# Gated expert stages: a tile's second product and the copy of its rows come one step later

## The chip, the cores and the metric

One core of one Trainium2 chip runs the whole program. The metric is the device time of one execution in microseconds; the kernel before has a median of 1701.94 us over three runs (1701.4 to 1706.82). Times inside the program come from one further execution, recorded by the hardware profiler.

## The reference

x is 32 x 128 tokens of 128 features, with a context of the same size. Four layers follow each other, each an attention over the context and then a mixture of eight experts, each added to x:

```python
x = x + _L0_xattn_ref(ctx_1024, _layernorm(x), ...)
x = x + _L0_ffn_ref(_layernorm(x), ...)      # top 2, GELU
x = x + _L1_xattn_ref(...)
x = x + _L1_ffn_ref(...)                     # top 2, gated, 256 rows an expert
x = x + _L2_xattn_ref(...)
x = x + _L2_ffn_ref(...)                     # top 2, gated
x = x + _L3_xattn_ref(...)
x = x + _L3_ffn_ref(...)                     # top 1, GELU
```

The two gated layers compute, for a token's row x and each chosen expert e, a product with two 128 x 256 matrices, a gate, and a product with a 256 x 128 matrix; the results of the chosen experts are mixed with the router's weights:

```python
# layer 1
y = a * (b * jax.nn.sigmoid(b)) @ W_out[e]   # a = xin @ W[e], b = xin @ V[e]
# layer 2
hidden = jax.nn.silu(gate_out) * up_out      # halves of x @ gate_up_w[e]
expert_out = hidden @ down_w[e]
```

## The kernel before

Rows are sorted by expert first, so that an expert stage works on tiles of 128 rows that all belong to one expert. `experts(layer)` (L1413) is that stage for all four layers. Layers 1 and 2 are `gated`. Layer 1 is also `fixed`: 16 tiles, two an expert, all indices known when the program is built. Layer 2 has up to 71 tiles (`n_tiles`), and which expert a tile belongs to is read from a table at run time, so its steps stand in a loop of eight, with a few steps written out before and behind (`run`, L1444).

The stage is a software pipeline, written out by hand as one function `step(k, u)` for each engine, where u is the slot of tile k among eight. Engines run by themselves and meet at semaphores; each works through its own program in order. In step k:

- PE (TensorE) turns the rows of tile k+2 (`turn_rows`, L1544, banks 0 and 1 of PSUM), makes the first product of tile k+1 (`hidden`, L1554, four matmuls of 128 x 128 in fp32, each seen as two records, into banks 2 and 3 or 4 and 5), and the second product of tile k (`rows_out`, L1566, two matmuls, four records, bank 6 or 7). Ahead of the first product it waits for DVE's copies of the tile's turned rows and of the expert's weights; ahead of the second for the gated features (`hidden_kept`) and for ACT's copy of the rows of two tiles before (`expert_kept`).
- ACT (ScalarE) applies Silu to the first half of tile k+1's first product (L1583) and then copies the finished rows of tile k-1 out of PSUM (L1594) into one of eight slots.
- DVE (VectorE) copies the turned rows of tile k+2 (L1626), in layer 2 the 128 x 512 weights of its expert into `tile_w1` (L1628), and then multiplies gate and second half of tile k+1 into `hidden` (L1633). In layer 1 it has preparations for the next attention in the same step (L1640, L1648).
- POOL (GpSimd) issues an indirect DMA for each tile that scatters its rows to DRAM (L1528). In layer 1 it also issues the indirect DMA that gathers a tile's rows (L1523), the gather of tile j ahead of the scatter of tile j-6. At the end it waits until all scatters have landed.
- SP (SyncE) in layer 2 loads the rows of tile j (L698), after the scatter of tile j-8 has landed, since that one reads its row numbers from the same slot. Ahead of the loads from tile 8 on stands a 2 MB load of the turned context (L1495).

The next stage's block starts when all engines have finished this one. Layers 0 and 3 use the same functions with four matmuls for the second product and GELU in place of the gate.

The order in PE's step and the two waits ahead of the second product:

```python
def step(k, u):
    turn_rows(k + 2, (u + 2) % SLOTS)
    hidden(k + 1, (u + 1) % SLOTS)
    rows_out(k, u)
...
pe.wait_ge(hidden_kept.sem, j + (hidden_kept.value + 1))
if beyond(j, 2):
    pe.wait_ge(expert_kept.sem, j + (expert_kept.value - 1))
```

Of the kernel before, what the change touches and what calls it, by code (L numbers as in the profile page):

```python
# [13 lines left out]
ALU = mybir.AluOpType  # L14
# [9 lines left out]
P = 128  # L24
# [4 lines left out]
H1 = 512  # L29
# [85 lines left out]
def build(nc, A, out):  # L115
    with ExitStack() as top:
# [1296 lines left out]
        def experts(layer):  # L1413
# [4 lines left out]
            NC = 2 if gated else 4  # L1418
            WIDE = H1 if gated else HB
            PARTS = 2  # L1420
            UNROLL = SLOTS
            LAG = 6
            scatters = layer in SCATTERED
# [3 lines left out]
            with ExitStack() as ph:  # L1427
# [1 line left out]
                xt = sb_in(ph, "tile_turned", [P, 2, P])  # L1429
                w1 = sb_in(ph, "tile_w1", [P, 4, WIDE])  # L1430
                gat = sb_in(ph, "gate", [P, 2, 2 * P])
                hidT = sb_in(ph, "hidden", [P, 2, NC * P])
                yo = sb_in(ph, "expert_rows_sb", [P, SLOTS, P])
                b2 = sb_in(ph, "expert_b2", [P, E * P])
                ctx_stats = sb_in(ph, "ctx_stats", [P, B, 6])
# [8 lines left out]
                def run(eng, step):  # L1444

                    if fixed:
                        for k in range(-2, n_tiles + 1):
                            step(k, k % UNROLL)
                        return
                    for k in range(-2, 2):  # L1450
                        step(k, k % UNROLL)
                    with eng.Fori(0, (n_tiles - 4) // UNROLL) as q:
                        for u in range(UNROLL):
                            step(q * UNROLL + (2 + u), (2 + u) % UNROLL)
                    for k in range(2 + (n_tiles - 4) // UNROLL * UNROLL, n_tiles + 1):
                        step(k, k % UNROLL)

                def in_slot(s):
# [8 lines left out]
                def slot_is_free(eng, j, s):  # L1467
                    if isinstance(j, int):
                        if j >= SLOTS:
                            eng.wait_ge(expert_out[s].sem, expert_out[s].value + 16 * (j // SLOTS))  # L1470
                    else:
                        eng.wait_ge(expert_out[s].sem, (j - s) * (16 // SLOTS) + expert_out[s].value)

                def hidden_bank(s, half):
                    return bank[2 + 2 * (s % 2) + half]
# [58 lines left out]
                def _(pe):  # L1534
# [11 lines left out]
                    def hidden(j, u):  # L1546
                        if exists(j):
                            pe.wait_ge(rows_turned_kept.sem, j + (rows_turned_kept.value + 1))
                            if not fixed:
                                pe.wait_ge(weights_placed.sem, j + (weights_placed.value + 1))  # L1550
                            for n in range(4):
                                c = (n + 2) % 4 if fixed else n
                                w = W1[:, (j // 2) * H1 + c * P:(j // 2) * H1 + (c + 1) * P] if fixed else w1[:, u % 4, c * P:(c + 1) * P]
                                ins = pe.matmul(hidden_bank(u, n // 2)[:, n % 2 * P:(n % 2 + 1) * P], w, xt[:, u % 2, :], start=True, stop=True)  # L1554
                                if n % 2:
                                    ins.then_inc(hidden_made.sem, 1)

                    def rows_out(j, u):
                        if exists(j):
                            off = expert_of(pe, j) * (NC * P)  # L1560
                            pe.wait_ge(hidden_kept.sem, j + (hidden_kept.value + 1))
                            if beyond(j, 2):
                                pe.wait_ge(expert_kept.sem, j + (expert_kept.value - 1))
                            out_ = bank[6 + u % 2]
                            for c in range(NC):
                                ins = pe.matmul(out_[:, 0:P], hidT[:, u % 2, c * P:(c + 1) * P], W2[:, bass.ds(off + c * P, P)],  # L1566
                                                start=(c == 0), stop=(c == NC - 1))
                            ins.then_inc(expert_made.sem, 1)

                    def step(k, u):  # L1570
                        turn_rows(k + 2, (u + 2) % SLOTS)
                        hidden(k + 1, (u + 1) % SLOTS)
                        rows_out(k, u)
                    run(pe, step)

                @block.scalar
                def _(act):
                    def step(k, u):
                        j, s = k + 1, (u + 1) % SLOTS
                        if exists(j):  # L1580
# [3 lines left out]
                            else:  # L1584
                                for c in range(NC):
                                    if c % 2 == 0:
                                        act.wait_ge(hidden_made.sem, j * PARTS + (hidden_made.value + 1 + c // 2))
                                    ins = act.activation(hidT[:, s % 2, c * P:(c + 1) * P], hidden_bank(s, c // 2)[:, c % 2 * P:(c % 2 + 1) * P], ACT.Gelu, bias=w1[:, s % 4, H1 + c:H1 + c + 1])  # L1588
                                ins.then_inc(hidden_kept.sem, 1)
                        j, s = k - 1, (u - 1) % SLOTS  # L1590
                        if gated and exists(j):
                            act.wait_ge(expert_made.sem, j + (expert_made.value + 1))
                            slot_is_free(act, j, s)
# [11 lines left out]
                def _(dve):  # L1605
# [8 lines left out]
                    def step(k, u):  # L1614
# [7 lines left out]
                        if exists(j):  # L1622
# [3 lines left out]
                            dve.tensor_copy(xt[:, s % 2, :], bank[s % 2][:, 0:P]).then_inc(rows_turned_kept.sem, 1)  # L1626
                            if not fixed:
                                dve.tensor_copy(w1[:, s % 4, :], W1[:, bass.ds(off, WIDE)]).then_inc(weights_placed.sem, 1)  # L1628
                        j, s = k + 1, (u + 1) % 2
                        if gated and exists(j):  # L1630
                            dve.wait_ge(gates_kept.sem, j + (gates_kept.value + 1))
                            dve.wait_ge(hidden_made.sem, j * PARTS + (hidden_made.value + 2))
                            dve.tensor_tensor(hidT[:, s, :], hidden_bank(s, 1)[:, 0:2 * P], gat[:, s, :], ALU.mult).then_inc(hidden_kept.sem, 1)  # L1633
                        if fixed and exists(k):
                            if k < QUARTERS * len(HEAD_PARTS):
                                whole, parts = HEAD_PARTS[k // QUARTERS]
# [1225 lines left out]
```

## Time and profile before

| what | value |
|---|---|
| median of three runs | 1701.94 us |
| lowest and highest | 1701.4 and 1706.82 us |
| profiled execution, first to last instruction | 1769.0 us |
| PE busy (share of the span) | 1426.5 us (81%) |
| PE weight loads busy | 1315.8 us (74%) |
| DVE busy | 1112.7 us (63%) |
| ACT busy | 892.0 us (50%) |
| POOL busy | 768.7 us (43%) |
| mean granted TensorE clock | 0.878 |

The profiled execution's span is the only time given of it; it is longer than the timed runs. Shares of busy time are means over stages that have different limits: the two gated stages are 51 us and some 145 us of the span. How a row is read: a group or a timeline row names the line of the kernel, the engine, the operation, what it writes and what it reads. "PEld" are PE's weight loads, which run beside its matmuls. Idle time is the engine's time with nothing running ahead of the row, and the arrow says whose semaphore came last. Starts are in us from the first instruction. A number of underscores behind a tile's name tells the stages apart: `hidden_` is layer 1, `hidden__` layer 2.

### The profile page before, as it was taken

The numbers are of one execution on the slowest core, as the hardware profiler recorded it, in microseconds if no ns is written. First come the engines' busy times: TensorE is split into PE (matmuls) and PEld (weight loads), VectorE is DVE, ScalarE is ACT, GpSimd is POOL, SyncE is SP. The second block draws the span as 40 slices with busy tenths as digits, with TensorE's granted clock in tenths as the row PEclk, the third lists the DMA queues.
The fourth block names the chain that finished last, engine by engine and source line by source line (L and its number), as shares of the span: only waits on it lengthen the run. The fifth ranks groups of instructions, "written<-read, shape, count | busy, mean of one in ns | idle before, by whom it ended". The sixth has DMA issues, their size and how long they took to land. (4 is left out here: it accounts for less than half of the span.)

```text
span 1769.0 us, 37485 instructions
## 1 busy us (share of the span) xinstructions
PE 1426.5 (81%) x10866; PEld 1315.8 (74%) x10867; DVE 1112.7 (63%) x3494; ACT 892.0 (50%) x2683; POOL 768.7 (43%) x764
## 2 busy tenths in 40 slices
PE   6665779975677569999999999999993999366494
PEld 4554579964556459999999999999992888154494
DVE  5634544438766457777777778787875455585343
ACT  4443135541223148777777777777771222243252
POOL 3064424430002545565656565666453455005342
PEclk9886779995576879999999999999997999677697
DMA  9311112213022130000000000000001322601224
GB/s 232 19 37 36 40 50 64 64 47 139 24 95 59 39 97 11 13 1 18 9 17 7 16 7 16 7 4 7 5 9 41 110 70 68 198 1 36 66 63 121
DMA packets 94444, 87.05 MB, mean 49 GB/s; under 512 B 17108, under 2 KB 81079, under 8 KB 93959
## 3 DMA queue, kind: packets, MB, share of 16 engines
q1 hardware_dynamic: 75240, 56.44, 12.1%
q0 software_dynamic: 11936, 24.55, 4.2%
q10 hardware_dynamic: 7168, 4.86, 1.0%
q8 instruction: 47, 0.77, 0.2%
q14 instruction: 53, 0.43, 0.1%
HBM read 54.03 MB, written 33.35 MB: 49 GB/s over the span
## 5 line engine op out<-in xcount | busy, mean ns | idle before, releaser
L2159 POOL TENSOR_TENSOR paired_rows<-paired_rows,rinv 128x1024 f32<-128x1024 f32 x128 | 242.4, 1894 | 245.1 <-DVE rinv L2474 230.3
L2465 DVE TENSOR_TENSOR probs_turned_lo<-psum_banks,probs_turned_hi 128x512 fp32r<-128x512 f32 x256 | 175.7, 686 | 141.9 <-ACT probs_turned_hi L2324 118.8
L2350 ACT ACTIVATE paired_rows<-psum_banks,neg_max 128x256 f32<-128x256 f32 x512 | 236.7, 484 | 1.1 <-DVEq L2051 0.4
L2271 PE MATMUL psum_banks<-probs_turned_hi,y_rows 128*128 128x256 f32 x1024 | 213.8, 292 | 0.9 <-DVEq L2051 0.9
L2221 PE MATMUL psum_banks<-y_turned_parts,queries_hi 128*128 128x256 f32 x1024 | 198.7, 292 | 3.0 <-DVEq L2051 3.0
L2271 PEld LDWEIGHTS psum_banks<-probs_turned_hi,y_rows 128*128 128x128 f32 x1024 | 167.1, 189 | 1.7 <-DVEq L2051 1.5
L2324 ACT CAST probs_turned_hi<-psum_banks 128x512 fp32r<-128x512 f32 x256 | 151.2, 591 | 20.4 <-PE psum_banks L2192 10.5
L2192 PE MATMUL psum_banks<-ident,paired_rows 128*128 128x128 f32 x1024 | 155.9, 275 | 6.9 <-DVE probs_turned_lo L2465 4.5
L2221 PEld LDWEIGHTS psum_banks<-y_turned_parts,queries_hi 128*128 128x128 f32 x1024 | 157.2, 190 | 3.5 <-issue 3.5
L2480 DVE TENSOR_REDUCE neg_max<-psum_banks 128x4 f32<-128x1024 f32 x128 | 155.5, 1215 | 5.5 <-PE psum_banks L2221 3.5
L2221 PE MATMUL psum_banks<-y_turned_parts,queries_lo 128*128 128x256 f32 x512 | 144.3, 282 | 0.0
L2271 PE MATMUL psum_banks<-probs_turned_lo,y_rows 128*128 128x256 f32 x512 | 144.2, 282 | 0.0
L2324 ACT CAST queries_hi<-psum_banks 128x512 fp32r<-128x512 f32 x128 | 74.9, 585 | 107.0 <-PE psum_banks L2257 94.9
L2192 PEld LDWEIGHTS psum_banks<-ident,paired_rows 128*128 128x128 f32 x1024 | 115.3, 140 | 11.9 <-DVE probs_turned_lo L2465 3.5
L1528 POOL DMA_INDIRECT expert_rows<-expert_rows_sb,tile_rows x71 | 70.9, 998 | 104.9 <-DVE expert_rows_sb L1620 104.9
L1588 ACT ACTIVATE hidden<-psum_banks,tile_w 128x128 f32<-128x128 f32 x284 | 81.2, 368 | 69.6 <-PE psum_banks L1554 69.6
L2350 ACT ACTIVATION_READ_ACCUMULATOR paired_rows<-psum_banks,neg_max 128x1 f32 x512 | 110.0, 215 | 0.0
L2257 PE MATMUL psum_banks<-y_turned_parts,wqk_hi 128*128 128x256 f32 x512 | 104.0, 296 | 0.8 <-POOL y_turned_parts L2083 0.8
L1528 POOL DMA_INDIRECT expert_rows<-expert_rows_sb__,tile_rows x71 | 68.3, 962 | 77.1 <-ACT expert_rows_sb__ L1594 64.8
L2271 PEld LDWEIGHTS psum_banks<-probs_turned_lo,y_rows 128*128 128x128 f32 x512 | 97.2, 190 | 0.0
L2221 PEld LDWEIGHTS psum_banks<-y_turned_parts,queries_lo 128*128 128x128 f32 x512 | 97.0, 189 | 0.0
L745 POOL DMA_INDIRECT rows_by_expert_first<-paired_rows,top_experts x64 | 62.1, 970 | 76.9 <-DVE top_experts L1123 45.0
(698 smaller groups left out, 3781.4 us busy)
## 6 DMA issues: line engine op xcount, KB each, us to landing
paired_rows<-expert_rows SPq DMA_DIRECT2D x16, 512.0 KB, 6.0
tile_rows<-rows_by_expert SPq DMA_DIRECT2D x110, 64.5 KB
tile_rows<-rows_by_expert_first SPq DMA_DIRECT2D x71, 64.5 KB
expert_w_b<-in_L_ffn_w_dram SPq DMA_DIRECT2D x2, 2048.0 KB, 12.9
tile_rows<-expert_rows SPq DMA_DIRECT2D x8, 512.0 KB
x_rows<-in_x_dram SPq DMA_DIRECT2D x8, 256.0 KB, 5.2
ctx_turned_dram<-ctx_turned SPq DMA_DIRECT2D x1, 2048.0 KB, 10.4
normed_rows_dram<-paired_rows SPq DMA_DIRECT2D x1, 2048.0 KB, 8.7
```

Source lines behind the costliest of these rows:

```text
L745: pool.indirect_dma_start(xfirst, bass.IndirectOffsetOnAxis(ap=first_spots[:, i, k, t:t + 1], axis=0), ROWS[:, i * N + t, :], None).then_i ...
L1528: pool.indirect_dma_start(ys, bass.IndirectOffsetOnAxis(ap=to, axis=0), yo[:, i % SLOTS, :], None).then_inc(expert_out[i % SLOTS].sem, 16)
L1588: ins = act.activation(hidT[:, s % 2, c * P:(c + 1) * P], hidden_bank(s, c // 2)[:, c % 2 * P:(c % 2 + 1) * P], ACT.Gelu, bias=w1[:, s % 4 ...
L2159: ins = pool.tensor_tensor(probs[:, k, :, :], probs[:, k, :, :], rinv[:, k, :].unsqueeze(2).to_broadcast([P, 4, 256]), ALU.mult)
L2192: ins = pe.transpose(bank[T_BANK][:, h * P:(h + 1) * P], probs[:, par, h, c * P:(c + 1) * P], ident[:, :])
L2221: ins = pe.matmul(bank[S_BANKS[par] + r][:, h * 256:(h + 1) * 256], queries[q][:, h, r, :], yparts[:, 2 * s2 + y, r * 256:(r + 1) * 256], ...
L2257: ins = pe.matmul(bank[Q_BANK][:, h * 256:(h + 1) * 256].rearrange("p (r q) -> p r q", r=2), wqk_parts[w][:, 2 * u3 + h, :], latents_of, s ...
L2271: ins = pe.matmul(bank[Z_BANK][:, r * 256:(r + 1) * 256], yrows[:, 2 * s1 + y, (2 * r + k) * P:(2 * r + k + 1) * P], probsT[x][:, (u + 1) ...
L2324: ins = act.copy(dst, bank[bank_][:, :])
L2350: ins = act.activation(probs[:, par, h, :], bank[S_BANKS[par] + h // 2][:, (h % 2) * 256:(h % 2 + 1) * 256], ACT.Exp, bias=nmax[:, par, h: ...
L2465: ins = dve.tensor_tensor(lo, bank[bank_][:, :], hi.bitcast(F32), ALU.subtract)
L2480: ins = dve.tensor_reduce(nmax[:, par, :], ps[:, S_BANKS[par]:S_BANKS[par] + 2, :].rearrange("p r (h k) -> p (r h) k", k=256), AX.X, ALU.m ...
```

## The change

For the gated layers PE's step k makes the second product of tile k-1 (it was k), and ACT's step copies the rows of tile k-2 (it was k-1). The gated features get four buffers (two before), and the first product of tile j waits in addition for the gated features of tile j-2 to be made, since the second product, by which this was ensured, no longer stands ahead of it. The stage has one step more at its end. Layers 0 and 3 keep their order and their waits.

```diff
--- before.py
+++ after.py
@@ -1418,6 +1418,7 @@
             NC = 2 if gated else 4
             WIDE = H1 if gated else HB
             PARTS = 2
+            BEHIND = 1 if gated else 0
             UNROLL = SLOTS
             LAG = 6
             scatters = layer in SCATTERED
@@ -1429,7 +1430,7 @@
                 xt = sb_in(ph, "tile_turned", [P, 2, P])
                 w1 = sb_in(ph, "tile_w1", [P, 4, WIDE])
                 gat = sb_in(ph, "gate", [P, 2, 2 * P])
-                hidT = sb_in(ph, "hidden", [P, 2, NC * P])
+                hidT = sb_in(ph, "hidden", [P, 2 + 2 * BEHIND, NC * P])
                 yo = sb_in(ph, "expert_rows_sb", [P, SLOTS, P])
                 b2 = sb_in(ph, "expert_b2", [P, E * P])
                 ctx_stats = sb_in(ph, "ctx_stats", [P, B, 6])
@@ -1444,7 +1445,7 @@
                 def run(eng, step):
 
                     if fixed:
-                        for k in range(-2, n_tiles + 1):
+                        for k in range(-2, n_tiles + 1 + BEHIND):
                             step(k, k % UNROLL)
                         return
                     for k in range(-2, 2):
@@ -1452,7 +1453,7 @@
                     with eng.Fori(0, (n_tiles - 4) // UNROLL) as q:
                         for u in range(UNROLL):
                             step(q * UNROLL + (2 + u), (2 + u) % UNROLL)
-                    for k in range(2 + (n_tiles - 4) // UNROLL * UNROLL, n_tiles + 1):
+                    for k in range(2 + (n_tiles - 4) // UNROLL * UNROLL, n_tiles + 1 + BEHIND):
                         step(k, k % UNROLL)
 
                 def in_slot(s):
@@ -1470,6 +1471,9 @@
                             eng.wait_ge(expert_out[s].sem, expert_out[s].value + 16 * (j // SLOTS))
                     else:
                         eng.wait_ge(expert_out[s].sem, (j - s) * (16 // SLOTS) + expert_out[s].value)
+
+                def hidden_slot(s):
+                    return s % (2 + 2 * BEHIND)
 
                 def hidden_bank(s, half):
                     return bank[2 + 2 * (s % 2) + half]
@@ -1548,6 +1552,8 @@
                             pe.wait_ge(rows_turned_kept.sem, j + (rows_turned_kept.value + 1))
                             if not fixed:
                                 pe.wait_ge(weights_placed.sem, j + (weights_placed.value + 1))
+                            if BEHIND and beyond(j, 2):
+                                pe.wait_ge(hidden_kept.sem, j + (hidden_kept.value - 1))
                             for n in range(4):
                                 c = (n + 2) % 4 if fixed else n
                                 w = W1[:, (j // 2) * H1 + c * P:(j // 2) * H1 + (c + 1) * P] if fixed else w1[:, u % 4, c * P:(c + 1) * P]
@@ -1563,14 +1569,14 @@
                                 pe.wait_ge(expert_kept.sem, j + (expert_kept.value - 1))
                             out_ = bank[6 + u % 2]
                             for c in range(NC):
-                                ins = pe.matmul(out_[:, 0:P], hidT[:, u % 2, c * P:(c + 1) * P], W2[:, bass.ds(off + c * P, P)],
+                                ins = pe.matmul(out_[:, 0:P], hidT[:, hidden_slot(u), c * P:(c + 1) * P], W2[:, bass.ds(off + c * P, P)],
                                                 start=(c == 0), stop=(c == NC - 1))
                             ins.then_inc(expert_made.sem, 1)
 
                     def step(k, u):
                         turn_rows(k + 2, (u + 2) % SLOTS)
                         hidden(k + 1, (u + 1) % SLOTS)
-                        rows_out(k, u)
+                        rows_out(k - BEHIND, (u - BEHIND) % SLOTS)
                     run(pe, step)
 
                 @block.scalar
@@ -1585,9 +1591,9 @@
                                 for c in range(NC):
                                     if c % 2 == 0:
                                         act.wait_ge(hidden_made.sem, j * PARTS + (hidden_made.value + 1 + c // 2))
-                                    ins = act.activation(hidT[:, s % 2, c * P:(c + 1) * P], hidden_bank(s, c // 2)[:, c % 2 * P:(c % 2 + 1) * P], ACT.Gelu, bias=w1[:, s % 4, H1 + c:H1 + c + 1])
+                                    ins = act.activation(hidT[:, hidden_slot(s), c * P:(c + 1) * P], hidden_bank(s, c // 2)[:, c % 2 * P:(c % 2 + 1) * P], ACT.Gelu, bias=w1[:, s % 4, H1 + c:H1 + c + 1])
                                 ins.then_inc(hidden_kept.sem, 1)
-                        j, s = k - 1, (u - 1) % SLOTS
+                        j, s = k - 1 - BEHIND, (u - 1 - BEHIND) % SLOTS
                         if gated and exists(j):
                             act.wait_ge(expert_made.sem, j + (expert_made.value + 1))
                             slot_is_free(act, j, s)
@@ -1626,11 +1632,11 @@
                             dve.tensor_copy(xt[:, s % 2, :], bank[s % 2][:, 0:P]).then_inc(rows_turned_kept.sem, 1)
                             if not fixed:
                                 dve.tensor_copy(w1[:, s % 4, :], W1[:, bass.ds(off, WIDE)]).then_inc(weights_placed.sem, 1)
-                        j, s = k + 1, (u + 1) % 2
+                        j, s = k + 1, (u + 1) % SLOTS
                         if gated and exists(j):
                             dve.wait_ge(gates_kept.sem, j + (gates_kept.value + 1))
                             dve.wait_ge(hidden_made.sem, j * PARTS + (hidden_made.value + 2))
-                            dve.tensor_tensor(hidT[:, s, :], hidden_bank(s, 1)[:, 0:2 * P], gat[:, s, :], ALU.mult).then_inc(hidden_kept.sem, 1)
+                            dve.tensor_tensor(hidT[:, hidden_slot(s), :], hidden_bank(s, 1)[:, 0:2 * P], gat[:, s % 2, :], ALU.mult).then_inc(hidden_kept.sem, 1)
                         if fixed and exists(k):
                             if k < QUARTERS * len(HEAD_PARTS):
                                 whole, parts = HEAD_PARTS[k // QUARTERS]
```

## Rows read from the trace of the kernel before

**Rows 1.** Busy time in two stretches: layer 1, layer 2's steady part; last clock, DMA.
```profile
562.00:613.00 51.00, 32.67 (x208) 29.07 (x208) 25.65 (x117) 14.40 (x41) 32.69 (x32) 0.82 0.14 41
1390.00:1503.00 113.00, 103.97 (x795) 93.23 (x794) 62.63 (x183) 33.05 (x123) 58.19 (x61) 1.00 0.25 70
```

**Rows 2.** Groups of lines, 1390 to 1503 us; busy, mean ns, then idle before, releasers.
```profile
L1554 PEld LDWEIGHTS psum_banks<-tile_turned__,tile_w__ 128*128 128x128 f32 x489 | 59.4, 191 | 9.7 <-DVE tile_w__ L1628 6.8 <-issue 2.6
...
L1566 PEld LDWEIGHTS psum_banks<-paired_rows,hidden__ 128*128 128x128 f32 x244 | 31.9, 190 | 9.3 <-issue 7.6
```

**Rows 3.** Timeline of PE, layer 2, two unstalled steps: start, length, what.
```profile
1411.72 1.06 PE L1554 MATMUL psum_banks<-tile_turned__,tile_w__ 128*128 128x128 f32 x8
...
1413.17 1.06 PE L1554 MATMUL psum_banks<-tile_turned__,tile_w__ 128*128 128x128 f32 x8
```

**Rows 4.** Timeline of all engines, layer 2, a stalled step.
```profile
1438.96 1.16 PE L1554 MATMUL psum_banks<-tile_turned__,tile_w__ 128*128 128x128 f32 x8
...
1440.81 1.06 PE L1554 MATMUL psum_banks<-tile_turned__,tile_w__ 128*128 128x128 f32 x8
1442.10 0.42 DVE L1633 TENSOR_TENSOR hidden__<-psum_banks,gate__ 128x256 f32<-128x256 f32 x1 [1.57 <-PE psum_banks L1554]
...
1442.77 0.71 PE L1566 MATMUL psum_banks<-paired_rows,hidden__ 128*128 x4 [0.91 <-DVE hidden__ L1633]
...
1443.12 0.44 DVE L1628 COPY tile_w__<-expert_w_a 128x512 f32 x1
...
1443.62 1.16 PE L1554 MATMUL psum_banks<-tile_turned__,tile_w__ 128*128 128x128 f32 x8
```

**Rows 5.** Groups of lines, layer 1, 562 to 613 us.
```profile
L1566 PEld LDWEIGHTS psum_banks<-expert_w_b,hidden_ 128*128 128x128 f32 x64 | 10.0, 222 | 7.1 <-DVE hidden_ L1633 3.9 <-issue 3.3
```

**Rows 6.** Instructions of L1566, whole span: duration ns min, median, max.
```profile
L1566 PEldq FUSED_REGOPS  x582: 46/46/65, 240.8 to 1743.3; - x194
```

**Rows 7.** Timeline, end of layer 2 and start of the next stage.
```profile
1505.52 0.38 ACT L1583 ACTIVATE gate__<-psum_banks 128x256 f32<-128x256 f32 x1 [2.10 <-PE psum_banks L1554]
...
1506.33 0.96 POOL L1528 DMA_INDIRECT expert_rows<-expert_rows_sb__,tile_rows  x1 [1.67 <-ACT expert_rows_sb__ L1594]
...
1508.86 0.95 POOL L1528 DMA_INDIRECT expert_rows<-expert_rows_sb__,tile_rows  x1 [0.30 <-DMA expert_rows<-expert_rows_sb__,tile_rows]
1517.54 0.31 SPq L2614 DMA_DIRECT2D mask_row<-mask_rows  x1
```

**Rows 8.** Timeline, end of layer 1: the first and last of three scatters.
```profile
609.48 0.96 POOL L1528 DMA_INDIRECT expert_rows<-expert_rows_sb_,pair_rows  x1 [0.93 <-ACT expert_rows_sb_ L1594]
...
612.00 0.95 POOL L1528 DMA_INDIRECT expert_rows<-expert_rows_sb_,pair_rows  x1 [0.30 <-DMA expert_rows<-expert_rows_sb_,pair_rows]
```

**Rows 9.** Timeline, start of layer 1: first two copies, first scatter.
```profile
573.19 0.26 ACT L1594 COPY expert_rows_sb_<-psum_banks 128x128 f32<-128x128 f32 x1
...
573.73 1.48 POOL L1528 DMA_INDIRECT expert_rows<-expert_rows_sb_,pair_rows  x1 [2.30 <-ACT expert_rows_sb_ L1594]
...
574.23 0.26 ACT L1594 COPY expert_rows_sb_<-psum_banks 128x128 f32<-128x128 f32 x1
```

**Rows 10.** Timeline, layer 2: scatters, loads, and turns of tiles 8 and 39.
```profile
1376.78 0.96 POOL L1528 DMA_INDIRECT expert_rows<-expert_rows_sb__,tile_rows  x1 [12.33 <-ACT expert_rows_sb__ L1594]
...
1378.23 0.96 POOL L1528 DMA_INDIRECT expert_rows<-expert_rows_sb__,tile_rows  x1 [0.49 <-issue]
...
1384.03 2.67 SPq L698 DMA_DIRECT2D tile_rows<-rows_by_expert  x3
...
1385.92 0.43 PE L1544 MATMUL psum_banks<-ident,tile_rows 128*128 128x128 f32 x1 [2.12 <-DMA tile_rows<-rows_by_expert]
...
1437.73 0.96 POOL L1528 DMA_INDIRECT expert_rows<-expert_rows_sb__,tile_rows  x1 [1.42 <-ACT expert_rows_sb__ L1594]
...
1440.12 0.33 SPq L698 DMA_DIRECT2D tile_rows<-rows_by_expert  x1
...
1445.19 0.27 PE L1544 MATMUL psum_banks<-ident,tile_rows 128*128 128x128 f32 x1
```

## The prediction

> **What bounds the kernel now.** I read the page first: span 1769.0 us, PE busy 81%. The slices show two kinds of stretch; the change touches only the gated expert stages, layer 1 (16 tiles, about 562 to 613 us) and layer 2 (71 tiles, about 1369 to 1510 us), so I cut the trace there. The windows show layer 2 in its steady part at full granted clock with PE busy 104.0 of 113 us, and layer 1 with PE busy 32.7 of 51 us beside POOL at 32.7 [rows 1]. PE "busy" is not the measure here: I counted tiles. The groups of lines give 244 second products of the steady part of layer 2, four a tile, so 61 tiles in 113 us, 1.85 us each; the weight loads sat idle 9.7 us before the first product (L1554) and 9.3 us before the second (L1566) [rows 2]. Where nothing stalls, PE starts the first product every 1.45 us [rows 3], which is 13 passes (one turn, eight, four) back to back. So 61 tiles need 88 us and about 24 us are lost. Half of what is visible stands ahead of L1566, the wait that the change aims at.
>
> Then the timeline of one bad step [rows 4]. The first product of tile 35 starts at 1438.96 and of tile 36 at 1440.81, both without a stall; but DVE gets to tile 35's gated multiply only at 1442.10, released by PE, 2 us after the modelled end of the matmuls that it reads. PE stands before L1566 until 1442.77 (0.91 idle, released by DVE's hidden). Then DVE copies the next turned rows and, at 1443.12, the next expert's weights (0.44), and the first product of tile 37 starts at 1443.62, behind that copy.
>
> The matmul end that this row shows is no measured end: the Trainium skill, "Perfetto Trace Analysis", section Tensor Engine Instruction, says that the profiler computes it from size and that the semaphore follows the write's acknowledgement. The row agrees (1440.12 modelled, reader at 1442.10).
>
> **Own time and the timed runs.** The page gives the profiled execution 1769.0 us between first and last instruction; the runs without a profile have a median of 1701.94 (1701.4 to 1706.82), 67 us less. Late completions such as the one above are my candidate for part of that; then layer 2 runs nearer to 1.45 us a tile when timed, and there is less to win than the trace shows. I work out the difference in the trace's time and put it on the median.
>
> **The change, part by part.**
>
> 1. Second product one step later (L1561 to L1568). In PE's order the step was: turn k+2, first product k+1, second product k; now the last is that of k-1, whose gated features are a whole step old. The wait for DVE's hidden goes: at most 9.3 us before L1566 in layer 2 and 7.1 us in layer 1 [rows 2, 5]. What is late next? DVE works in order: multiply of tile k, turned rows of k+2, weights of k+2. None of these moves. In [rows 4] the multiply at 1442.10 is released by the first product, not by the second; from it to the end of the weights copy is 1443.12 + 0.44 - 1442.10 = 1.46 us, while PE's released second product plus turn ask 4 + 1 of the 13 passes, 0.56 us, after a multiply of 0.42 and a wake-up of 0.25 (1442.52 to 1442.77), 1.23 us in all. So when the multiply is late, the first product of k+2 is later still by 0.2 to 0.3 us, whatever PE did before. If the second product of 34 runs at 1441.7 instead, PE just stands 1.1 us longer before L1554 and starts tile 37 at 1443.62 all the same. Bounds for the gain in layer 2: 0 (all taken over by the weights wait) and 9.3 us; I take 0, since the row measured is this very case. In layer 1 the same with the turned rows in place of the weights, and there POOL paces the stage (two indirect DMAs a tile, one every 1.26 us as in rows 8, so 2.5 us a tile against PE's 1.45): bounds 0 and 7.1, taken 0.
>
> 2. The added wait in hidden() on hidden_kept of j-2. It guards the two banks of the first product. DVE did that multiply before it placed the weights of j (rows of j in layer 1), for which PE waits on the line before, so it never ends last. Queued behind it is PE's whole stream. Price: one or two sequencer operations, 46 ns each of the kind seen at L1566 [rows 6]; 0 if the sequencer is ahead of the array, 0.09 x 87 = 8 us if it is not. In the unstalled steps the matmuls follow each other without a gap [rows 3], so I take 0.
>
> 3. ACT's copy one step later. ACT's step is gate k+1, then the copy, now of k-2. The copy waits for nothing new; PE's second product still waits for a copy that stands behind the same gate as before, so its bank wait is neither better nor worse. But the scatter on POOL waits for the copy. At the end this is on the path: in layer 2 gate 70 at 1505.52 is followed by the copy of 68, and three scatters stand from 1506.33 to 1508.86, one every 1.26, and the next stage starts at 1517.54 only after the last has landed [rows 7]. Now the copy of 67 is behind that gate too: four scatters in a row instead of three, +1.26 us. Bounds 0 (if the last product came later than the queue) and 1.26; I take 1.26, because the queue is what is waited for.
>
> 4. The same at layer 1's end: three scatters from 609.48 to 612.00 behind gate 15 become four, +1.26 [rows 8]. At its start POOL idles 2.30 us for the first copy (573.19) before scatter 0; the second copy is at 574.23, and that is where the first now stands: POOL +1.04 [rows 9]. Behind scatter 0 in POOL's order is the gather of tile 7, which PE reaches several us later. If POOL is saturated to the end, the 1.04 carries through and the 1.26 does not; if not, the reverse. I take 1.3 for layer 1; bounds 0 and 2.3.
>
> 5. SP's loads in layer 2 wait for the scatter of eight tiles before. Scatter 0 goes from 1376.78 to about 1378.23, where scatter 1 stood; load 8 was issued at 1384.03, and the turn of tile 8 at 1385.92 waited for it with PE idle 2.12 us [rows 10]. The 2 MB copy of the turned context fills the DMA engines between, and scatter 1 was home by the time SP came to load 9 (1.2 us later). So 0 to 1.2 us, taken 0.3. In steady state a load follows its scatter by 2.39 us (1437.73 to 1440.12) and lands in 1.89 (1384.03 to 1385.92): 4.3 us needed [rows 10]. The turn of tile 39 was at 1445.19 [rows 10], 7.5 us after scatter 31; less one tile (1.85) leaves 5.6. Hidden, at this pace.
>
> 6. Four buffers for the features: 2 KB more a partition and no instruction; 0.
>
> Sum: 0 + 0 + 1.26 + 1.3 + 0.3 = **+2.9 us**, 1771.9 in the trace's time, **1704.8 us** for the median. That is 0.17%, under the 0.3% (5.1 us) that a measurement of this kernel can tell from no change.
>
> **Rivals.**
>
> A. *The wait removed pays.* For: 9.3 us stand before L1566, as many as before L1554, and the multiply that releases it is one of the longest steps. Against: the takeover shown in rows 4. If layer 2's 9.3 come off in full, 2.9 - 9.3 = -6.4: 1695.5 us; with layer 1's 7.1 as well 1688.4. The Trainium skill, "Trainium Kernel Development and Optimization", section Best Practices, speaks for it: consistent bubbles can mean that SBUF or PSUM ran out, and here buffers go from two to four. The trace agrees on bubbles, and names a copy, not a buffer, for those before L1554; by the page the time would be this rival's.
>
> B. *The slot cycle decides (slower).* Place: eight row slots of layer 2, scatter k, load k+8, turn k+8. The 7.46 us of part 5 are four tiles of 1.85; at 1.45 a tile they are 5.85, and less one tile 4.4, against 4.3 needed. Point of decision: a pace below about 1.45 us, or a landing only 0.1 us slower. Short by 0.45 over three remaining tiles is 0.15 a tile, x 63 = 9.5; with the 2.9, 1714 us. For: the timed runs are faster than the trace. Against: in the trace PE never waits for a load after tile 8.
>
> C. *PE's sequencer*: part 2's 8 us, with 2.9: 1712 us.
>
> D. *The order does nothing* and the ends hide behind the drain of the block: 1702 us.
>
> **How the numbers follow.** Chances: forecast 0.50 (of which 0.03 beyond 0.3%), D 0.03, A 0.24, B 0.18, C 0.05. Faster 0.24; same 0.47 + 0.03 = 0.50; slower 0.03 + 0.18 + 0.05 = 0.26. The forecast's own range is 1700 to 1708 (bounds of parts 3 to 5). For 8 in 10 it reaches to the middle of A and of B: 1692 to 1714.
>
> **What would show it.** Right: idle before L1566 in layer 2 falls towards 1 us, idle before L1554 grows by about as much, the period stays at 1.85; four scatters in a row at both ends. Wrong: a steady part of layer 2 shorter by 5 us or more (A); PE or its loads waiting for tile_rows after tile 8 (B); a fast period above 1.45 us (C). My step 1 fails if the first product's start moves with the second's.

## The result, and the profile after

The kernel after takes 1709.46 us (median of 20, 1702.22 to 1717.17) against 1703.2 us of the kernel before (median of 20); the ratio is 1.0038, 95% interval 1.0023 to 1.0053: 6.5 us slower, 3.9 to 9.0. One execution of the kernel before took 2400.04 us and is not in the ratio; its others took 1697.37 to 1708.91. Added to the 1701.94 us that I started from, 6.5 us make 1708.4: inside my wide range (1692 to 1714), just outside the forecast's own (1700 to 1708), and on the slower side of the 0.3% line. My point was 2.9 us slower.

The profiled execution says the opposite: its span is 1708.4 us against 1769.0 of before. I therefore read the profile of after by what it says of itself, and take differences from the experiments. ("Undisturbed" below is a trace whose span agrees with its timed runs, as all of them do but that of 1769.0 us.) The windows of the gated stages of the kernel after (columns as in rows 1):

```profile
530.00:573.00 43.00, 28.50 (x208) 25.37 (x208) 25.74 (x117) 12.97 (x38) 29.87 (x32) 0.93 0.17 48
1340.00:1445.00 105.00, 101.70 (x800) 95.15 (x799) 63.63 (x184) 32.97 (x122) 59.09 (x62) 0.98 0.29 82
```

This window has 61 tiles in 105 us, 1.72 us each, against 1.85 [rows 1, 2]; but it begins earlier in the stage than that of rows 1. From the tenth turning to the last a tile takes 1.64 us. The groups of weight loads in that window:

```profile
L1560 PEld LDWEIGHTS psum_banks<-tile_turned__,tile_w__ 128*128 128x128 f32 x494 | 61.1, 195 | 2.4 <-DVE hidden__ L1639 0.3 <-issue 0.2
L1572 PEld LDWEIGHTS psum_banks<-paired_rows,hidden__ 128*128 128x128 f32 x244 | 32.3, 193 | 2.2 <-issue 0.4
L1548 PEld LDWEIGHTS psum_banks<-ident,tile_rows 128*128 128x128 f32 x61 | 8.7, 143 | 5.3 <-DMA tile_rows<-rows_by_expert 4.2
```

The idle ahead of the second product fell from 9.3 to 2.2 us, and that ahead of the first product, which I said would take it over, from 9.7 to 2.4 [rows 2]. Before the turning of the rows stand 5.3 us, 4.2 of them released by the rows' load. Most of this is one wait, for tile 8 behind the 2 MB load, and that one stood in the kernel before too (2.12 us [rows 10]), ahead of the window of rows 1:

```profile
1344.65 0.33 PE L1548 MATMUL psum_banks<-ident,tile_rows 128*128 128x128 f32 x1 [2.92 <-DMA tile_rows<-rows_by_expert]
```

Behind it, from 1346 us on, 1.1 us in four waits are left for the load. They are the mark that I had given for rival B, and a small one. Layer 2's end is as forecast. Timeline of layer 2's end; the first gate shown is the last of the stage:

```profile
1449.87 0.38 ACT L1589 ACTIVATE gate__<-psum_banks 128x256 f32<-128x256 f32 x1 [0.81 <-PE psum_banks L1560]
...
1450.68 0.96 POOL L1532 DMA_INDIRECT expert_rows<-expert_rows_sb__,tile_rows  x1 [0.39 <-ACT expert_rows_sb__ L1600]
1450.94 0.27 ACT L1600 COPY expert_rows_sb__<-psum_banks 128x128 f32<-128x128 f32 x1 [0.53 <-PE psum_banks L1572]
1451.95 0.96 POOL L1532 DMA_INDIRECT expert_rows<-expert_rows_sb__,tile_rows  x1 [0.30 <-issue]
...
1453.21 0.96 POOL L1532 DMA_INDIRECT expert_rows<-expert_rows_sb__,tile_rows  x1 [0.30 <-issue]
1454.47 0.96 POOL L1532 DMA_INDIRECT expert_rows<-expert_rows_sb__,tile_rows  x1 [0.30 <-DMA expert_rows<-expert_rows_sb__,tile_rows]
1463.16 0.31 SPq L2620 DMA_DIRECT2D mask_row<-mask_rows  x1
```

Four scatters stand behind the gate, where three did, and from the gate to the next stage's first load are 13.29 us, where 12.02 were [rows 7]. At layer 1's start GpSimd stood 2.74 us for the first copy, and the second came 1.90 us behind it:

```profile
539.74 0.26 ACT L1600 COPY expert_rows_sb_<-psum_banks 128x128 f32<-128x128 f32 x1
540.28 0.99 POOL L1532 DMA_INDIRECT expert_rows<-expert_rows_sb_,pair_rows  x1 [2.74 <-ACT expert_rows_sb_ L1600]
...
541.64 0.26 ACT L1600 COPY expert_rows_sb_<-psum_banks 128x128 f32<-128x128 f32 x1
```

### The profile page after: what moved, and what is told of

It is laid out like the page before. It is cut to its first block and busy times, and to the rows that moved or that the text cites. A ratio compares the mean times of both kernels' runs of the same rounds, so it can differ in the third digit from the quotient of the medians.

```text
span 1708.4 us, 37557 instructions
## 1 busy us (share of the span) xinstructions
PE 1407.8 (82%) x10866; PEld 1305.0 (76%) x10867; DVE 1114.5 (65%) x3494; ACT 893.2 (52%) x2683; POOL 768.2 (45%) x764
## 3 DMA queue, kind: packets, MB, share of 16 engines
q1 hardware_dynamic: 75240, 56.44, 12.3%
## 5 line engine op out<-in xcount | busy, mean ns | idle before, releaser
L1548 PE MATMUL psum_banks<-ident,tile_rows 128*128 128x128 f32 x197 | 57.2, 291 | 49.0 <-PEq L1947 15.7
```

The lines of the kernel that those rows point to most:

```text
L1548: pe.transpose(bank[u % 2][:, 0:P], xr[:, u, 0:P], ident[:, :]).then_inc(rows_turned.sem, 1)
```

## The experiments

A difference of 6 us in 1700 is at the edge of what timing resolves, and the profile of before was unlike its timed runs. So I ran the stage of one layer six times inside the kernel and read the differences between such kernels. "Five stages" below is the time in the trace from the first turned tile of the second run of the stage to the last of the sixth. The four kernels of experiment 1 ran on one chip, the four of experiment 2 on a second, those of experiments 3 and 5 on a third and the one of experiment 4 on a fourth. The unchanged kernel took 1700.0, 1703.9, 1700.8 and 1703.3 us there, so timed medians of different groups compare to some 5 us only, and I rest on the traces.

**1. Which layer, and is it the profile or the kernel?** Four kernels: before and after, layer 2 or layer 1 six times.

```diff
         experts(2)
+        for _ in range(5):
+            experts(2, True)
...
```

> The kernel before with the stage of layer 2 run six times in a row (the same rows, the same results; the repeats load all their tiles themselves and leave the 2 MB context load out). It gives the stage's time without a profile: the excess over the kernel before, divided by five. My estimate from the unstalled steps of the trace is 71 x 1.45 = 103 us plus some 15 us of filling, draining and barrier, about 120 us a stage, so about 2300 us in all. If the stage ran timed as it ran in the trace (1.85 us a tile), it would be about 150 us a stage and 2450 us.

> The changed kernel with the stage of layer 2 six times. Against the same of before: the forecast's terms give 6 x 1.26 (one more scatter in the row at the end) + 0.3 + 1.3 (layer 1, once) = +9 us. If the removed wait pays: 6 x -9.3, about -50 us. If the slot cycle of scatter, load and turn decides: 0.1 to 0.15 us a tile, +40 to +65 us. If PE's sequencer pays for the added wait: 71 x 6 x 0.09, +38 us. If all of the measured 6.5 us lies in layer 2: +39 us.

> The kernel before with the stage of layer 1 run six times (the five rehearsals write the low parts of the next attention's weights to a scratch tile). It gives the stage's time without a profile. By POOL's 32 indirect DMAs at 1.26 us, 5 x (40 + 10) = +250 us over the kernel before.

> The changed kernel with the stage of layer 1 six times. Against the same of before: the forecast gives 6 x 1.3 + 1.6 = +9 us. If the removed wait pays in layer 1: 6 x -7.1, about -40 us. If all of the measured 6.5 us lies in layer 1: +39 us.

Layer 2: 2330.2 us (2326.8 to 2338.6) and 2368.5 (2360.5 to 2377.7), ratios to the kernel before 1.3701 [1.3618, 1.3783] and 1.3932 [1.3849, 1.4015]. A stage of before takes 126 us, where I had estimated 120. The medians are 38.3 us apart, 6.4 us a stage; the traces give less, 29.7 us from the first turning of the first stage to the first of the next layer, 4.9 us a stage. The profiled spans, 2327.4 and 2358.8, agree with the timed runs, so a profile does not by itself cost 67 us: the 1769.0 us execution was a disturbed one. Groups of one repeated stage, before (1594 to 1690 us) and after (1605 to 1705 us):

```profile
L1554 PEld LDWEIGHTS psum_banks<-tile_turned____,tile_w____ 128*128 128x128 f32 x496 | 60.2, 192 | 0.5
L1566 PEld LDWEIGHTS psum_banks<-paired_rows,hidden____ 128*128 128x128 f32 x250 | 32.8, 191 | 1.8 <-issue 0.2
L1544 PEld LDWEIGHTS psum_banks<-ident,tile_rows 128*128 128x128 f32 x62 | 8.8, 143 | 0.9 <-issue 0.2
```

```profile
L1560 PEld LDWEIGHTS psum_banks<-tile_turned____,tile_w____ 128*128 128x128 f32 x496 | 60.3, 191 | 2.3 <-DVE hidden____ L1639 0.5 <-issue 0.3
L1572 PEld LDWEIGHTS psum_banks<-paired_rows,hidden____ 128*128 128x128 f32 x248 | 32.4, 190 | 1.8 <-issue 0.2
L1548 PEld LDWEIGHTS psum_banks<-ident,tile_rows 128*128 128x128 f32 x62 | 8.8, 142 | 1.7 <-DMA tile_rows<-rows_by_expert 1.0
```

Ahead of the second product the weight loads sit idle 1.8 us a stage with before's code, not 9.3, and as much after; none of it is put down to the gated features. So the wait that the change removes was worth next to nothing. One cycle of a slot of the rows in either kernel: scatter k, load k+8 (SyncE), turning k+8. Before:

```profile
1650.18 0.96 POOL L1528 DMA_INDIRECT expert_rows<-expert_rows_sb____,tile_rows  x1 [0.58 <-ACT expert_rows_sb____ L1594]
...
1652.66 0.34 SPq L698 DMA_DIRECT2D tile_rows<-rows_by_expert  x1
...
1656.53 0.27 PE L1544 MATMUL psum_banks<-ident,tile_rows 128*128 128x128 f32 x1
```

and after:

```profile
1650.33 0.96 POOL L1532 DMA_INDIRECT expert_rows<-expert_rows_sb____,tile_rows  x1 [0.50 <-ACT expert_rows_sb____ L1600]
...
1652.72 0.33 SPq L698 DMA_DIRECT2D tile_rows<-rows_by_expert  x1
...
1655.22 0.27 PE L1548 MATMUL psum_banks<-ident,tile_rows 128*128 128x128 f32 x1
```

Scatter to load is 2.5 and 2.4 us. Load to turning is 3.87 before and 2.50 after; from tile 16 on the medians are 3.65 and 2.40 us. After, in the steady part, every fourth turning comes 1.8 to 2.0 us behind its load, which is the shortest there is in these traces; the three behind it follow at 2.3 to 2.5. So 1.8 us of margin are left before, and after none at every fourth tile. Four such turnings of the stage show the wait itself, the longest here:

```profile
1701.80 0.14 PEld L1548 LDWEIGHTS psum_banks<-ident,tile_rows 128*128 128x128 f32 x1 [0.34 <-DMA tile_rows<-rows_by_expert]
```

Layer 1 by time says nothing: 1966.0 us (1956.0 to 1974.7) before, 1954.3 (1952.8 to 1961.6) after; in the profiled execution of before another stage lost 27 us (last section). (Before lies 266 us above the unchanged kernel, where I had expected 250.) By the trace, the six stages take 269.6 us before and 281.6 after, first to last turned tile: 2.0 us a stage more.

**2. The added wait, alone and left out; and the copy moved.** Three suspects for layer 2's steady part: the slot cycle (B), the wait's instruction (C), the new order itself (called E).

```diff
# l2x6_before_wait; l2x6_after_nowait takes the same wait out of the kernel after
...
+                            if gated and beyond(j, 2):
+                                pe.wait_ge(hidden_kept.sem, j + (hidden_kept.value - 1))
```

```diff
# l2x6_before_cf (here) and l2x6_after_cf: ACT's step, ahead of the gate of k + 1
+                        j, s = k - 1, (u - 1) % SLOTS
+                        if gated and exists(j):
+                            act.wait_ge(expert_made.sem, j + (expert_made.value + 1))
+                            slot_is_free(act, j, s)
+                            act.copy(yo[:, s, :], bank[6 + s % 2][:, 0:P]).then_inc(expert_kept.sem, 1)
                         j, s = k + 1, (u + 1) % SLOTS
...
-                        j, s = k - 1, (u - 1) % SLOTS
...
```

> The kernel before with layer 2's stage run six times, as in l2x6_before (2330.2 us), and with the change's added wait alone: in every step of the gated stages TensorE waits for hidden_kept of an earlier tile ahead of its first product. The wait is for a count that is long reached, so only the instruction is added. Theory C (the wait's own instruction on TensorE's sequencer makes the step longer, 0.055 to 0.06 us a tile as between the traces of l2x6_before and l2x6_after): about 2355 us, six times 71 steps by 0.058 us above l2x6_before. Theory B (the copy that comes a step later frees the slot of the rows a step later, and the load of the rows arrives late): 2330, no change. Theory E (the order of the two products itself costs the 0.06 us, by the new gap between the steps): 2330, no change.

> The kernel after with layer 2's stage run six times, as in l2x6_after (2368.5 us), without the added wait ahead of the first product (the wait for the copy of the weights, which VectorE makes behind the multiply of the tile two before, stands in for it). Theory C: all of the steady-state loss goes, 2343 us, of which 7 us above l2x6_before are the longer ends (six by 1.16 us). Theories B and E: 2368, no change.

> The kernel before with layer 2's stage run six times, and ScalarE's copy of a tile's rows put ahead of its gate of the next tile in both gated stages, so that a scatter is issued up to half a step earlier. Theory B: the rows' loads come earlier by as much, and what is left in the kernel before of waits for them goes; 2 to 6 us a six stages below 2330. Theory C: 2330 in the steady state. Against both, the gate and with it the multiply come later by the copy's 0.2 to 0.3 us; if the way from first product through gate and multiply to second product is what binds, it is slower by up to 71 by 6 by 0.2 = 85 us. I expect 2330, within 8 us.

> The kernel after with layer 2's stage run six times, and ScalarE's copy of the rows put ahead of its gate in both gated stages. In this order of work the second product of tile k-1 is issued behind the first product of tile k+1, so the gate has a whole step more of room, and the copy of tile k-2 is ready to go long before. Theory B: the scatter comes about half a step earlier, and half or more of the 0.06 us a tile goes: 2345 to 2355. At the ends a copy ahead of the last gate saves up to 1.16 us a stage, 7 us. Theory C: only the ends gain, 2361. Theory E: the same 2361.

**3. Sixteen slots.** The five repeated stages get sixteen slots, for the rows and for the finished rows, and sixteen steps in a turn of the loop, so the load of tile k waits for the scatter of k-16. Both kernels of the pair have all of this.

```diff
...
+            SLOTS = 16 if again else 8
...
+                xr = sb_in(ph, "tile_rows_16", [P, SLOTS, P + 1]) if again else tile_rows
...
```

> The kernel before with layer 2's stage run six times, of which the five repeated stages have sixteen slots for the rows (and sixteen steps in a turn of the loop) in place of eight; the first stage keeps eight. The row load of tile k then waits for the scatter of tile k-16 and no longer for that of k-8. Theory B (the cycle of the slots): the kernel before has 1.2 us of margin on its loads (3.65 us from a load's issue to its turning against 2.4 where the turning waits for it), so that only its load waits now and then go. What also goes is half of the turns of the loop, with about 0.5 us each (the steps of 1.68 and 1.77 us in each eight): 1.50 us a tile in the repeated stages in place of 1.56, about 2310 us.

> The kernel after with layer 2's stage run six times, of which the five repeated stages have sixteen slots and sixteen steps in a turn of the loop. Theory B: the cycle no longer binds, a load is issued some 12 us ahead of its turning, and the repeated stages run at the same time a tile as those of l2x6_before_s16; above that kernel stay six ends of 1.16 us and the first stage's 2 us: 9 us, so about 2319. Theory E (the order of the two products or the new wait costs the 0.06 us a tile by itself): the repeated stages stay 4 us each above those of l2x6_before_s16, 31 to 38 us in all.

All eight, layer 2 six times: timed median; then from the trace, in us, the five stages, a tile's mean in them, last turned tile to the first of the next stage, and the median from a load's issue to its turning, from tile 16 on.

```
                    timed    five stages   a tile   to next   load to turn
l2x6_before        2330.2       614.0      1.562     16.8        3.65
l2x6_before_wait   2343.6       624.4      1.592     16.8        3.73
l2x6_before_cf     2319.8       606.6      1.548     16.2        4.22
l2x6_before_s16    2327.7       607.5      1.539     17.2       15.5
l2x6_after         2368.5       638.6      1.618     18.1        2.40
l2x6_after_nowait  2369.2       637.1      1.613     18.1        2.30
l2x6_after_cf      2343.8       618.9      1.569     17.4        2.94
l2x6_after_s16     2336.7       613.3      1.542     18.4       14.1
```

What follows. *C is out as the cause*: without the wait the kernel after is as slow (2369.2). Put into the kernel before it costs 0.03 us a tile in the trace and 13 us in time, but the intervals of the ratios overlap (1.3633 to 1.3807 and 1.3618 to 1.3783), and l2x6_after_s16 carries the same wait and runs at 1.542 us a tile; what it costs alone stays open. *B is shown twice.* Half a step of earlier scatters gives the kernel after 19.7 us back in its five stages, and its tiles come to 1.569; the same edit gives the kernel before 7.4 us, so 12.3 us are what after gains beyond it. Its 2343.8 us lie just below the 2345 to 2355 that theory B had asked for. (I had expected the kernel before at 2330 within 8, and 2 to 6 us below by theory B; it took 2319.8.) Sixteen slots take the loss away altogether: 1.542 against 1.539 us a tile. E had asked for 31 to 38 us between these two; timed, they are 9.0 us apart, B's number, and 1.2 us a stage of that are the ends. So the order of the products and the new wait, which the kernel after keeps here, cost nothing to speak of. Group of the rows' turning in a repeated stage of l2x6_after_s16 (1600 to 1691 us), where the load is gone from the releasers:

```profile
L1550 PEld LDWEIGHTS psum_banks<-ident,tile_rows_ 128*128 128x128 f32 x59 | 8.4, 143 | 0.3
```

My totals for the pair were wrong: 2310 and 2319 expected, 2327.7 and 2336.7 measured. In its five stages l2x6_before_s16 gained 6.6 us, not 20: the halved turns of the loop gave less than I had counted (1.54, not 1.50 us a tile), the gaps between stages grew by 0.4, and in its trace layer 2 begins 3.8 us later than in l2x6_before, before any sixteen slots are used.

**4. Layer 1: GpSimd's queue.** In layer 1 GpSimd issues 32 indirect DMAs, 1.28 us apart in the median, and hardly pauses; with LAG 6 the eighth gather is queued behind the first scatter, and so behind the first copy. Experiment: one gather more ahead of it.

```diff
...
-            LAG = 6
+            LAG = 7 if fixed else 6
...
```

> The kernel after with layer 1's stage run six times, as in l1x6_after (1954.3 us), with LAG 7 in place of 6 in layer 1: GpSimd issues the gather of tile 7 (the eighth) ahead of the first scatter, not behind it. Theory P (in layer 1 GpSimd's own queue binds: 32 issues of about 1.27 us a stage, and the change only makes its wait for the first copy longer, from 1.0 to 2.0 us up to 2.7 to 3.7): a gather fills 1.25 us of this wait in each stage, so the six stages from first to last turned tile take about 274 us in place of 281.5 (269.5 in l1x6_before), and the time is about 1946. Rival: the end of a stage (one copy and scatter more in a row) is what costs the 2 us a stage; then nothing moves, 281 and 1954.

Measured 1944.0 us (1940.8 to 1946.0) against 1954.3, on another chip; six stages 268.7 us in the trace, against 269.6 before and 281.6 after. From its first gather to its last scatter GpSimd needs 42.3 us a stage in l1x6_before, 44.3 in l1x6_after and 42.2 here. Theory P holds against its rival, by which nothing would have moved; but 12.9 us came back where it asked for 7.5, more than the change had cost (12.1). The kernel before with LAG 7 was not run, so how much of the gain any kernel would have from it is open. GpSimd's first scatter of the first stage in l1x6_before, l1x6_after and l1x6_after_lag7:

```profile
534.21 0.99 POOL L1529 DMA_INDIRECT expert_rows<-expert_rows_sb_,pair_rows  x1 [1.01 <-ACT expert_rows_sb_ L1595]
```

```profile
536.27 0.98 POOL L1533 DMA_INDIRECT expert_rows<-expert_rows_sb_,pair_rows  x1 [2.87 <-ACT expert_rows_sb_ L1601]
```

```profile
542.56 0.98 POOL L1533 DMA_INDIRECT expert_rows<-expert_rows_sb_,pair_rows  x1 [1.77 <-ACT expert_rows_sb_ L1601]
```

Between the first two the wait grows by 1.86 us; in the third 1.1 of it is filled. (Its stage begins later, so only the brackets compare.) Over the six stages the wait is 1.53 us in the mean before, 3.04 after and 1.70 with LAG 7. These 1.5 us are what a stage grew between its first and last turning; the other 0.5 to 0.6 of layer 1's 2.0 lie between the last turning and the next stage's first.

**5. The moved copy by itself, each layer once.** The edit of `_cf` on the kernel before, without the change.

> The kernel before, each layer once, with ScalarE's copy of a tile's rows ahead of its gate of the next tile in both gated stages, and nothing of the change. By l2x6_before_cf against l2x6_before (2319.8 against 2330.2 us over six stages) layer 2 gives 1.7 us, and layer 1 at the most 1 or 2 more: 1700 us, 2 to 3 us below the kernel before. If the gate, now behind the copy, were late for the second product, it would be slower instead, 71 tiles by the copy's 0.2 us: 1717.

1698.6 us (1694.9 to 1702.5, 12 runs) against 1700.8 (17 runs), ratio 0.9989 [0.9967, 1.001]: the size expected, and not to be told from no change. No kernel here is shown to beat the one before.

## Why the prediction was off by half, point by point

The forecast of a small loss held, in part by luck: of the 6.5 us only layer 2's end came as I had put it. The largest part came from rival B, to which I had given 0.18, and the 0 for the removed wait was right for a wrong reason.

**Steps 1 and 2 (removed wait, added wait), taken 0: right in size, the first for a reason that did not apply.** I argued that the weights' copy takes the removed wait over, from rows 4. In undisturbed executions the wait is not there to be taken over: 1.8 us a stage ahead of L1566 with before's code, 0.5 ahead of L1554, and in layer 1 no idle at all ahead of L1566, where rows 5 have 7.1. Rows 2, 4 and 5 belong to one execution in which the multiply of layer 2 began up to 2.0 us behind the modelled end of the matmuls that it reads, and over 1 us in 15 of 54 tiles. In the undisturbed traces of before and after it is 0.11 us in the median. I had 67 us between this execution and the timed runs before me, and named late completions as a candidate; I should have gone on to distrust every idle time that rested on them. Rival A, the removed wait pays, had its 9.3 us from the same rows, and it fell for that.

**Step 3 (layer 2's end), 1.26 us: right.** From 16.8 to 18.1 us in the mean of the gaps between repeated stages.

**Step 5 (slot cycle), taken 0.3: this is the step that failed.** The 0.3 was for tile 9, behind the 2 MB load; the steady part I put at nothing, "hidden, at this pace", and the pace was the disturbed 1.85 us. The steady part measured 3.9 us in a repeated stage, (1.618 - 1.562) x 70, and 3.3 us in the stage as the kernel has it once (first to last turning 115.4 us in the mean of three traces with before's code, 113.5 to 116.9, and 118.8 in five with after's, 117.3 to 119.7). A slot of the rows goes round a ring: turning, copy, scatter, load, next turning, eight tiles later. Its length, as I estimate it from the traces: a tile's copy starts three steps and 1.04 us behind its turning before, four steps and 1.04 us after; 0.54 to the scatter, 2.40 to the load, 1.9 to a turning that waits. That is 5.9 us beside the steps. Eight steps must hold it all: five are left for it before, 5.9 / 5 = 1.2 us each, and four after, 5.9 / 4 = 1.5. The tile in four that does wait takes 6.3 (1.3, 0.54, 2.6 and 1.9), 1.6 a tile. The rest of the kernel runs at 1.54 to 1.56. So the change took the ring from well under the pace up to it, where every late landing is paid, and 1.618 was measured. Why one tile in four takes the longer way is open. That is rival B, its place and point of decision as put there. Its price was too high (0.15 us a tile, 1714 us): it rests on a shortfall of 0.45 us that its own rows do not give (4.4 us there against 4.3 needed), and on a pace of 1.45 that before itself did not reach (1.56: two steps in eight are longer).

**Step 4 (layer 1), 1.3: mechanism half right, size 2.0.** I had bounded it by start (1.04) and end (1.26) and said that a saturated GpSimd would carry the first. It does, and the start cost 1.5 in the mean of six stages (1.9 in the first): the first two copies stand 1.90 us apart in the profile after, and 1.87 in l1x6_before, where rows 9, of the disturbed execution, have 1.04.

**Step 6 (feature buffers), 0:** nothing in any trace speaks against it; it was not run by itself. Rivals C and D: C by l2x6_after_nowait no cause of the loss; D fell with the ends. The rule that I had weighed for rival A, of the Trainium skill, "Trainium Kernel Development and Optimization", section Best Practices (consistent bubbles can mean that SBUF or PSUM ran out), is borne out in the kernel after, for another buffer than I read it for: with twice the feature buffers the 1.8 us ahead of the second product stayed as they were, and with twice the slots of the rows the load's wait went away.

Sum as measured in the traces: 3.3 (layer 2's cycle) + 1.2 (its end) + 2.0 (layer 1) = 6.5 us, against 6.5 [3.9, 9.0] timed. That the two agree so well is chance: single traces of one code differ by up to 3.4 us in layer 2 alone.

## What to carry to other kernels

Moving a consumer a step later lengthens every ring that runs through it. Before counting what it hides, add up the ring (compute, copy, store, reload) and divide by its slots; the step is free only while that stays below the pace of the undisturbed kernel, and that pace is to be taken from a trace whose span agrees with the timed runs. To find 6 us in 1700, repeat the stage and compare stages within traces.

## What the runs showed of the hardware that I had not expected

One execution can be longer by 60 us (1769.0 against 1708.4 and the timed 1697 to 1709) and say nothing of the kernel. Here at least 27 us of it lie ahead of the first expert stage's first turning (at 232 us, against 195 to 206 in the thirteen other traces) and some 17 in layer 2 (133.1 us against 113.5 to 116.9), while the long attention between layers 1 and 2 took 763 us as elsewhere. What disturbed it is open.

A loop whose code is fetched again in every turn can cost more than the whole change. In l1x6_before the attention after layer 1 took 789 us from layer 1's last turning to layer 2's first, against 760 to 765 in every other trace of these kernels. Set beside l2x6_before, matmul by matmul, it falls behind at four places alone, by 7.0, 6.6, 5.9 and 7.3 us, about 93 us apart. At each, TensorE stands idle twice ahead of L2195, 1.8 to 2.0 us and then 2.2 to 2.8, in wait of nothing that the profile names, and the other engines fall idle too. Its granted clock is still at 2.4 GHz in the first idle time and falls to 1.2 GHz ahead of the second one's end, for 3.4 or 6.8 us. Windows ahead of the first place, in the first idle time and at the low clock (columns as in rows 1), then TensorE's rows:

```profile
1080.00:1095.00 15.00, 14.89 (x132) 14.54 (x130) 12.91 (x37) 11.38 (x35) 5.69 (x3) 1.00 0.01 3
1096.00:1098.00 2.00, 0.43 (x2) 0.31 (x3) 0.00 (x0) 0.00 (x0) 0.00 (x0) 1.00 0.03 8
1098.60:1105.40 6.80, 5.90 (x28) 5.86 (x28) 3.27 (x5) 2.24 (x5) 3.31 (x4) 0.50 0.01 2
```

```profile
1096.83 0.43 PE L2195 MATMUL psum_banks<-ident,paired_rows 128*128 128x128 f32 x2 [1.94 <-issue]
1099.50 0.37 PE L2195 MATMUL psum_banks<-ident,paired_rows 128*128 128x128 f32 x1 [2.24 <-issue]
```

So the low clock follows the idle time and is not what began the loss. The DMA queue that brings instructions shows what differs. In l1x6_before it moves 31 packets between 1100 and 1430 us:

```profile
q8 instruction: 31, 0.51, 0.7%
```

In the same 345 us of the attention, 295 to 640 us behind layer 1's last turning, this trace has 34 such packets and each of the thirteen others has none. That the idle times are waits for code fits this; no run tests it, and why this one program fetches its loop again is open. In this execution the four places outweigh the 12 us by which layer 1's stages were faster, and turn the comparison with l1x6_after around.
